# Attention turns with the value products issued between the scores and the shifted scores

## The reference, cut to what matters

```python
q, k, v = (proj(w_q), proj(w_k), proj(w_v))
scores = jnp.einsum('bhqd,bhkd->bhqk', q, k) * SCALE
probs = jax.nn.softmax(scores, axis=-1)
attn = jnp.einsum('bhqk,bhkd->bhqd', probs, v)
```

## Time and profile before

| | us |
|---|---|
| median of three runs | 858.49 |
| lowest, highest | 856.21, 858.85 |
| the profiled execution | 861.54 |
| its span, first to last instruction | 859.8 |
| PE busy in the span | 786.1 (91%) |
| DVE busy | 603.0 (70%) |
| ACT busy | 444.6 (52%) |
| POOL busy | 407.9 (47%) |

### The profile page before, as it was taken

One profiled execution on the slowest core, in us unless ns is written; L12 is line 12 of the kernel. 1 busy time (PEld: TensorE's weight loads), 2 busy tenths in 40 slices (PEclk: granted clock), 3 DMA queues, 4 the chain that ended last, 5 costly groups with the idle time before them and its releaser, 6 DMA issues.

```text
span 859.8 us, 16650 instructions
## 1 busy us (share of the span) xinstructions
PE 786.1 (91%) x5918; PEld 651.1 (76%) x5918; DVE 603.0 (70%) x1317; ACT 444.6 (52%) x758; POOL 407.9 (47%) x595
## 2 busy tenths in 40 slices
PE   7699989999989976887999999999999999999993
PEld 6577767766766653576889898898898888988983
DVE  4757888888788885673756856756657568665992
ACT  3166767767666765632434534434345435343670
POOL 1002255555555546447046445254464462556674
PEclk9889999999999997899899999999999999999997
DMA  6567775555555561316045245253352351533741
GB/s 163 120 155 161 145 173 113 114 114 114 114 123 116 112 163 53 124 29 184 13 89 109 42 89 114 49 124 50 80 115 40 92 111 31 147 50 59 285 178 46
DMA packets 71582, 92.49 MB, mean 108 GB/s; under 512 B 13276, under 2 KB 55933, under 8 KB 71372
## 3 DMA queue, kind: packets, MB, share of 16 engines
q1 hardware_dynamic: 53964, 68.48, 31.3%
q0 software_dynamic: 16928, 22.15, 14.8%
q10 hardware_dynamic: 608, 0.79, 0.4%
HBM read 39.18 MB, written 26.62 MB: 77 GB/s over the span
## 4 chain that ended last, share of the span: by engine, by line
PE 68%; DVE 15%; issue 6%; another core or an unknown queue 4%; POOL 3%; ACT 2%; DMA 1%; SPq 0%; POOLq 0%; ACTq 0%; DVEq 0%
PE bank L1699 15%; DVE negm L884 10%; PE wide L1668 8%; PE wide L1666 8%; PE wide L1667 8%; PE bank L1701 8%; PE bank L972 7%; PE wide L1017 6%; PE bank L1645 2%; PE wide L1035 2%; PE bank L1082 2%; PE bank L981 1%; PE bank L1051 1%; POOL out L1401 1%
## 5 line engine op out<-in xcount | busy, mean ns | idle before, releaser
L1345 POOL DMA_INDIRECT acc_rows<-o_w,lists x70 | 120.4, 1720 | 184.0 <-ACT o_w L1489 170.6
L884 DVE TENSOR_REDUCE negm<-wide 128x4 f32<-128x1024 f32 x128 | 156.0, 1222 | 47.1 <-PE wide L1017 30.7
L633 ACT ACTIVATE probs<-wide 128x1024 f32<-128x1024 f32 x128 | 130.8, 1024 | 85.6 <-PE wide L1035 64.8
L1456 ACT ACTIVATE h<-wide,b1T 128x512 f32<-128x512 f32 (+1 forms) x200 | 115.0, 601 | 104.1 <-PE wide L1668 70.1
L1701 PE MATMUL bank<-stack,h_lo 128*128 128x256 f32 x560 | 156.9, 280 | 0.0
L1666 PE MATMUL wide<-g_hi,stack 128*128 128x512 f32 (+1 forms) x400 | 141.7, 354 | 7.2 <-issue 3.9
L1667 PE MATMUL wide<-g_lo,stack 128*128 128x512 f32 (+1 forms) x400 | 141.1, 353 | 0.4 <-issue 0.4
L1668 PE MATMUL wide<-g_hi,stack 128*128 128x512 f32 (+1 forms) x400 | 141.2, 353 | 0.2 <-issue 0.2
L1489 ACT ACTIVATE o_w<-o_b,lists 128x256 f32<-128x256 f32 x70 | 35.7, 510 | 148.6 <-DVE o_b L1627 139.9
L1699 PE MATMUL bank<-stack,h_hi 128*128 128x512 f32 x304 | 108.5, 401 | 0.0
L1701 PEld LDWEIGHTS bank<-stack,h_lo 128*128 128x128 f32 x560 | 105.6, 189 | 0.0
(11 more groups left out here) (208 smaller groups left out, 1640.7 us busy)
## 6 DMA issues: line engine op xcount, KB each, us to landing
stack<-qk SPq DMA_DIRECT2D x186, 128.0 KB, 4.2
w_raw<-in_L_ffn_w SPq DMA_DIRECT2D x16, 1024.0 KB
x_sb<-in_L_attn_x SPq DMA_DIRECT2D x16, 256.0 KB, 5.0
x_rows<-x SPq DMA_DIRECT2D x16, 256.0 KB
acc_rows<-x SPq DMA_DIRECT2D x16, 256.0 KB
acc_sb<-acc_rows SPq DMA_DIRECT2D x8, 512.0 KB, 12.3
out<-acc_sb SPq DMA_DIRECT2D x8, 512.0 KB
x_rows<-zrow SPq DMA_DIRECT2D x2, 1024.0 KB, 5.9
```

Of the source, the lines that this page charges most:

```text
L633: nc.scalar.activation(probs[:, i % 4].rearrange("p x c t -> p x (c t)"), shifted_banks(i)[:, :, :], ACT.Exp, scale=SCALE).then_inc(exp_do ...
L884: nc.vector.tensor_reduce(negm[n % 2][:, :, :, u].rearrange("p c x -> p x c"), score_banks(PAIRS * n + u)[:, :, :].rearrange("p x (c t) -> ...
L1345: nc.gpsimd.indirect_dma_start(out=acc_d, out_offset=bass.IndirectOffsetOnAxis(ap=lists[:, e, QC * c + r, 0:1], axis=0), in_=o_w[c][:, r, ...
L1456: ins = nc.scalar.activation(h[u % 2][:, t], banks[BZ[u % 4]][:, t], ACT.Relu, bias=b1T[:, FT * e + f:FT * e + f + 1])
```

## The change

In PE's program for the turns, the block that issues the value products moves up: it stood behind the shifted scores, the transposes of the maxima and those of the value sums, and now stands between the scores and the shifted scores. Waits and matmuls inside the block are the same, and the programs of the other engines are untouched.

```diff
@@ -1056,6 +1056,10 @@
                 if p is not None:
                     scores(*p)
+                for t in range(QUADS):
+                    m = due(turn, PV0 + 2 * t, NB)
+                    if m is not None:
+                        pv(m, t)
                 p = pair_of(turn, ST0, NB)
                 if p is not None:
                     shifted_scores(*p)
@@ -1082,10 +1086,6 @@
                     ins.then_inc(uT_ready, 1)
-                for t in range(QUADS):
-                    m = due(turn, PV0 + 2 * t, NB)
-                    if m is not None:
-                        pv(m, t)
                 n = due_after(turn, XT1, XT, NB)
```

## The result

The changed kernel takes **913.67 us** (median of five runs, 907.41 to 917.17) against 858.35 of the kernel before in five (856.21 to 858.85): the ratio is 1.0631, 95% interval 1.0592 to 1.0669, so it is slower by 55 us. The prediction was 903 us, with a range of 884 to 918 and a chance of 0.97 for slower. The profiled execution took 913.67 us with a span of 911.9, 52.1 us more than the profiled one of before.

What follows compares the result with a forecast made beforehand. Odd turns were taken as bound by DVE's maximum, even turns by PE. First group 2.5, twelve groups at 3.25 (39.0) and last three 3 sum to 44.5 us over the 858.49 median: 903 us, range 884 to 918.

Steps and rivals of the forecast that it cites:

- The chain: Odd turn's scores, value products, shifted scores, exponential, up to the next turn's shifted scores: 3.06 us, before 2.18 to 2.23.
- First pair: First odd and even turn of an eight-turn group: PE stalls 0.88 us before the even turn's shifted scores.
- second: Second pair of turns in a group: PE stalls 0.83 us before the even turn's shifted scores.
- fourth: Fourth pair of turns in a group: PE stalls 0.83 us before the even turn's shifted scores.
- Third pair: Pair around GpSimd's list writes, the uncertain term: 0.71 us more, between -0.32 and +1.77.
- the late signals: Third pair: PE's finish signals seem to arrive late around GpSimd's list writes; moved scores' signal also seen only at 216.84.
- The first and last groups: First of 16 groups: 2.5 us, one pair free; last three together: 3 us (0 to 6).
- The low one (887): Second rival, third pair: signals are prompt for scores moved from their old place; 887 us, chance 0.10.
- the high one (918): First rival, third pair: late signals move with PE's order rather than the list writes; 918 us, chance 0.11.
- The clock, given 0.04: Third rival: three of twelve attention groups run at PE's lower clock, 44 us on top; 947 us, chance 0.04.
- a clock that drops in the stretch 120 to 200: Sign against the forecast: PE's granted clock, 1.00 in these 80 us of attention turns before, drops there.
- the fourth rival: Not slower: the even turn's wait is covered because the maximum releases the next scores; 844 to 858 us, chance 0.03.

Runs made afterwards that it cites:

- undisturbed pair of kernels: Old and new order, each with a sequence's four list writes spread over four even turns: 846.2 us (0.9807 of before) and 895.94 us (1.0349).
- last turns alone: Kernel before with value products ahead of the shifted scores only from turn 129 on: 864.9 us, ratio 1.0057 to before.
- no list writes: Old and new order without the indirect DMAs writing the first 12 sequences' list entries: 840.47 us (0.9743 of before) and 899.49 us (1.0404).
- first odd turn's: Kernel before with value products ahead only in each group's first odd turn (8k + 1), below turn 129: 889.66 us, ratio 1.032.
- third odd turn's runs: Kernel before with value products ahead only in each group's third odd turn (8k + 5), below turn 129: 897.31 us, ratio 1.0415.

## Why the prediction was right

**The mechanism.** The shifted scores behind the value products delay the exponential, the even turn's shifted scores wait for it, and the projections behind them on PE pay. The chain was forecast at 3.06 us and measured 3.06 in the first pair of turns; shortening the exponential by 0.42 shortened it by 0.43 and every pair of a group without list writes by 0.41 to 0.43. Of the signs named beforehand, an odd turn keeps its length (1.83 us against 1.84), its exponential begins 1.98 us behind its scores in place of 0.80, and a group grows by 3.6 us on average, where 3.3 were forecast.

**The terms of the sum.** First pair 0.88 forecast, 0.98 measured; second 0.83 against 0.89; fourth 0.83 against 0.90. What failed there is small: the shifted scores, alone on PE after their wait, hold up what follows by 0.43 us, where before it was 0.33 to 0.38. Third pair 0.71 forecast; it measures 0.99 where no list is written, 0.3 on average (-0.1 to 0.6) in the six groups with list writes and a steady clock (5.97 against 5.73 in that of turn 73), since both orders then wait for the late signals, and 1.2 to 1.9 in the four where the clock falls. The forecast had the reason right (the moment is tied to the list writes, which the runs without them show) and no term for the clock. That the mean over the twelve groups, 0.85, comes near 0.71 is luck: the falls of the clock, which the sum put at nothing, gave back what the late signals swallow. Over twelve groups all pairs make 43.0 us against 39.0. The undisturbed pair of kernels splits that: by the starts of the scores of turns 33 and 129 the new order takes 268.3 and the old 223.1 us with spread writes, 45.2 for the chain alone; the list writes add 14.8 to the old order and 12.5 to the new.

**The first and last groups** were put at 2.5 and 3. The first measures (67.20 - 47.06) - (64.61 - 47.42) = 2.95, worked out from the scores of turns 25 and 33. The stretch from turn 129 on measures 6.6 in the profiled execution, just over its bound of 0 to 6; between other traces that differ by the order there it is 0.7 (last turns alone) to 13.5 us (no list writes), so its size is not settled. The spans thus differ by 52.1 us where 44.5 were forecast; the medians differ by 55, since the profiled execution of before was 3 us over its median and that of the changed kernel is its median.

**The rivals.** The low one (887) and the high one (918) differed in when the late signals come, and the 913.67 measured is nearer to 918 than to 903, so the time alone would not tell them apart. The rows of the third pair in the changed kernel do (scores, the last list write, their maximum, the next scores; the group's first scores go at 182.53):

```profile
194.13 0.50 PE L1017 MATMUL wide<-stack 48*128 48x256 f32 x4
194.33 0.97 POOL L531 DMA_INDIRECT slot_list<-item,dest  x1 [0.30 <-issue]
...
196.40 1.23 DVE L884 TENSOR_REDUCE negm<-wide 128x4 f32<-128x1024 f32 x1 [2.14 <-remote]
...
197.68 0.50 PE L1017 MATMUL wide<-stack 48*128 48x256 f32 x4 [1.62 <-DVE negm L884]
```

The maximum begins 13.87 us after the group's first scores, where before it was 216.84 - 202.64 = 14.20, although PE's order has moved: the late signals end with the list writes, as forecast, and those of the moved scores are not prompt. So neither is what happened, though the first odd turn's and the third odd turn's runs show how dear a third pair can get. The clock, given 0.04 as a cause for 947 us, took part: it fell in four of the twelve groups for about 1.5 us each (7.47 - 5.97), and more in the last turns. One sign that the prediction gave for being wrong, a clock that drops in the stretch 120 to 200, has thus come:

```profile
120.00:200.00 80.00, 67.51 (x667) 49.98 (x666) 56.31 (x138) 47.70 (x79) 36.49 (x85) 0.98 0.43 92
```

It stands at 0.98 where it was 1.00. The prediction kept the 2.4 GHz level because its stalls were all under 2.2 us, beside the 4.52 us hole; that reason failed. (The 1.22 us wait that it counted among the idle time of 120 to 200 before lies at 218.12, outside; the longest in that stretch is 1.24, at 137.73.) The third pair shows the fall at waits of 1.6 us and the same wait without it:

```profile
173.04 0.79 PE L1017 MATMUL wide<-stack 48*128 48x256 f32 x4 [1.61 <-DVE negm L884]
...
197.68 0.50 PE L1017 MATMUL wide<-stack 48*128 48x256 f32 x4 [1.62 <-DVE negm L884]
```

0.79 us at the lower level, 0.50 at the upper, behind the same wait. The section of the Trainium skill that the prediction weighed ("TensorE: Matmul & The Clock Gate", "A second HAM failure mode: psum-queue depth-cycling") is borne out in part: the clock swings between its two levels in these rows. But where stalls of 0.6 to 0.7 us come in every even turn and nothing else, with spread writes, the clock stays at 1.00 over 269 us: frequent short idle times alone did not bring it down there. Not slower, the fourth rival, is excluded.

## What to carry to other kernels

A block that waits for nothing new can still cost: moved ahead of an instruction that feeds another engine, it lengthens the loop through that engine by its own length, and the price is paid wherever the next round of that loop stands at the head of a queue that has no slack. Issue first what another engine is waiting for, and put what only this engine needs behind it. And before parts of a change are added up, see whether a stall also moves the clock: one of four moved blocks cost 31 or 39 us here, all four 55.

## What the runs showed of the hardware

Around indirect DMAs that GpSimd issued 1.3 us apart, PE's finish signals reached ACT and DVE about 2 us late (1.9 to 2.2 us in the rows above), while PE itself went on and DVE's signals were prompt (in the changed kernel the maximum of 196.40 ends at 197.63, and PE goes on at 197.68); the profile can only call it "remote". Left out or issued one to an even turn, the delay was gone in every group (third pair 5.73 to 4.25 us). Why the signals are held was not settled.

PE's clock was at its lower level in stretches behind some of those waits and not behind others of equal length. Neither the new order nor the list writes are needed for that. With the last turns alone moved, where the groups have the old order, the third pair of the group of turn 57 took 8.48 us, with a wait of 2.54 us and a granted clock of 0.85 over the group; and in the first group, before any list is written, the clock fell there at 62.0, after a wait of 1.09 us that ended at 59.75 (0.88 over that group), while the kernel before has the same wait until 59.85 and kept 1.00. The time of the changed kernel spread over 10 us (907 to 917), that of the undisturbed one of the new order over 6 (891.54 to 897.34); that the clock makes the difference is likely, but not shown.
